# An eight-layer transformer block on one core: a deformable-attention loop's broadcasts, edge turns and warm-up matmuls reordered, and a product's last piece given to GpSimd

## The reference, cut to what matters

```python
x = x + _L0_xattn_ref(...)
...
x = x + _L2_xattn_ref(ctx_1024, ctx_1024, _layernorm(x, axis=-1), mask, Wk, bk, Wv, bv, Wq, bq, Woff, boff, Wo, bo)
...
x = x + _L3_ffn_ref(_layernorm(x, axis=-1), w_gate, w_up, w_down)
```

## Time and profile before

| | us |
|---|---|
| median of 3 runs | 460.71 (460.51 to 461.78) |
| the profiled execution, its own time | 460.47 |
| its span in the trace | 458.4 |
| PE busy | 396.8 |
| DVE busy | 360.2 |
| ACT busy | 253.6 |
| POOL busy | 111.7 |

### The profile page before, as it was taken

The page is one execution under the profiler, slowest core; times in us unless marked ns, Lnnn a source line. Parts: engine busy times, 40 slices in busy tenths (PEclk is TensorE's granted clock), DMA queues, the critical chain, the costliest instruction groups (busy, mean ns, idle before and its releaser), DMA issues.

```text
span 458.4 us, 8682 instructions
## 1 busy us (share of the span) xinstructions
PE 396.8 (87%) x3411; PEld 260.9 (57%) x3411; DVE 360.2 (79%) x807; ACT 253.6 (55%) x443; POOL 111.7 (24%) x92
## 2 busy tenths in 40 slices
PE   8988989999999988877787888899999999868156
PEld 5555556566666667643454555476656866643045
DVE  5799646548544487989699888998899799987985
ACT  4785753323223335377688785776667433444952
POOL 3200000006990001005993543131211023100200
PEclk9999999999999999999899999999999999989759
DMA  7990000000000000027000003000000000000001
GB/s 232 358 322 6 1 1 1 1 0 1 0 0 1 1 1 4 0 62 307 1 2 0 3 1 70 0 2 1 1 0 1 3 1 1 3 0 0 1 1 46
DMA packets 11084, 16.51 MB, mean 36 GB/s; under 512 B 5274, under 2 KB 9764, under 8 KB 10148
## 3 DMA queue, kind: packets, MB, share of 16 engines
q1 hardware_dynamic: 10756, 15.17, 9.5%
q10 hardware_dynamic: 288, 0.79, 0.5%
HBM read 15.43 MB, written 0.52 MB: 35 GB/s over the span
## 4 chain that ended last, share of the span: by engine, by line
PE 47%; DVE 34%; ACT 10%; issue 7%; DMA 1%; POOL 0%; ACTq 0%; DVEq 0%
PE ps L852 7%; PE ps L857 7%; PE ps L891 7%; PE ps L2156 5%; DVE arena L1937 3%; PE ps L2146 2%; PE ps L1786 2%; DVE stats L252 2%; DVE arena L2405 1%; DVE arena L2402 1%; DVE arena L610 1%; DVE arena L613 1%; PE ps L242 1%; DMA ctx_fm<-in_ctx_fm 1%; DVE arena L2433 1%
## 5 line engine op out<-in xcount | busy, mean ns | idle before, releaser
L970 DVE SCALAR_TENSOR_TENSOR arena<-ps,cols,arena 128x512 f32<-128x512 f32 x40 | 29.7, 750 | 42.3 <-PE ps L857 38.0
L866 ACT ACTIVATE arena<-ps,cols 128x512 f32<-128x512 f32 x40 | 27.4, 687 | 63.9 <-PE ps L852 63.8
L242 PE MATMUL ps<-const 128*128 128x256 f32 x158 | 42.2, 414 | 7.4 <-ACT arena L2746 4.4
L891 PEld LDWEIGHTS ps<-weights,arena 128*128 128x128 f32 x320 | 38.6, 192 | 8.1 <-issue 8.0
L1937 DVE TENSOR_SCALAR arena<-ps 128x512 f32<-128x512 f32 x56 | 36.4, 683 | 7.1 <-PE ps L1772 3.8
L242 PEld LDWEIGHTS ps<-const 128*128 128x128 f32 x158 | 30.8, 205 | 16.1 <-ACT arena L2746 4.7
L891 PE MATMUL ps<-weights,arena 128*128 128x128 f32 x320 | 39.2, 276 | 0.2 <-DVE x_tm L959 0.2
L857 PE MATMUL ps<-h_fm,weights 128*128 128x512 f32 x80 | 37.7, 593 | 0.7 <-DVE arena L970 0.7
L852 PE MATMUL ps<-h_fm,weights 128*128 128x512 f32 x80 | 37.7, 594 | 0.6 <-ACT h_fm L373 0.6
L2146 PE MATMUL ps<-h_fm,weights 128*128 128x512 f32 x64 | 30.3, 606 | 2.7 <-ACT arena L2530 1.8
L1772 PE MATMUL ps<-l2buf,picks_b 128*128 128x256 bf16 x160 | 25.6, 277 | 5.8 <-DVE arena L1937 4.8
(11 more groups left out here) (408 smaller groups left out, 884.4 us busy)
## 6 DMA issues: line engine op xcount, KB each, us to landing
weights<-in_moe_w SPq DMA_DIRECT2D x2, 2048.0 KB, 10.1
weights<-in_moe_w SPq DMA_DIRECT2D x3, 1280.0 KB
l2buf<-in_picks SPq DMA_DIRECT2D x1, 1664.0 KB, 7.6
rows<-in_rows SPq DMA_DIRECT2D x1, 1024.0 KB, 13.7
x_tm<-in_x SPq DMA_DIRECT2D x2, 256.0 KB, 5.0
ctx_fm<-in_ctx_fm ACTq DMA_DIRECT2D x1, 512.0 KB, 5.7
ctx_tm<-in_ctx SPq DMA_DIRECT2D x1, 512.0 KB, 14.5
mats<-in_mats SPq DMA_DIRECT2D x1, 512.0 KB, 14.8
```

The costliest lines, as they stand in the source:

```text
L242: PE.matmul(ps[:, bank, 0:256], ident, const[:, 0:256], start=True, stop=True)
L866: AC.activation(silu[:, k, :], ps[:, k, :], ACT.Silu, bias=bias_col(0, e, k)).then_inc(silu_ok, 1)
L891: ins = PE.matmul(ps[:, 4 + u % 2, P * t:P * t + P], glu[:, u % 2, k, P * t:P * t + P], w3[:, e, k, :], start=(k == 0), stop=(k == 1))
L970: V.scalar_tensor_tensor(out=glu[:, u % 2, k, :], in0=ps[:, 2 + k, :], scalar=bias_col(1, e, k), in1=silu[:, k, :], op0=ALU.add, op1=ALU.m ...
```

## The change

1. First attention: `stay_busy(pe, 2, 6)` is issued at t = 0 and at t = 1.
2. PE in the deformable loop: `sample(0)` comes after all five broadcasts of step 0. In step 1 the order is broadcast 5, one call of `stay_busy`, `move(2)`, broadcasts 6 to 9. The edge's turn comes after the step's broadcasts, just ahead of its `sample`.
3. ACT in the loop: `keep_positions(2)` comes ahead of the ramp of step 1; `keep_edge` comes after the ramps and `keep_values`.
4. DVE in the loop: the split of the third group of positions comes after hat 2 of step 0, ahead of hat 3.
5. Last product: ACT rounds in four pieces (512, 512, 1024, 1024 columns), and also subtracts the magic for the last 512 columns; POOL multiplies these 512 columns; DVE multiplies the other 2560 in four pieces and takes four maxima in all (the first two pieces in one). `gt_ok` reaches 6 after the third of four pieces, and the 8 calls of `stay_busy` start there.

```diff
-                    if t == 0:
+                    if t in (0, 1):
                         stay_busy(pe, 2, 6)
...
                     if w in MOVE_STEPS[3:]:
                         move(pe, MOVE_STEPS.index(w))
-                    if w in EDGE_STEPS:
-                        turn_edge(pe, EDGE_STEPS.index(w))
                     if w % 2 == 0 and chunks(w):
                         pe.wait_ge(ix_ok, w // 2 + 2)
                     for c in chunks(w)[:3]:
                         broadcast(w // 2 + 1, c)
-                    if w == 0:
-                        sample(0)
-                    if w == 1:
-                        move(pe, 2)
+                        if w == 1 and c == chunks(w)[0]:
+                            stay_busy(pe, 1, 6)
+                            move(pe, 2)
                     if w >= 2:
                         turn(w - 2)
                     for c in chunks(w)[3:]:
                         broadcast(w // 2 + 1, c)
+                    if w in EDGE_STEPS:
+                        turn_edge(pe, EDGE_STEPS.index(w))
+                    if w == 0:
+                        sample(0)
                     if 0 < w < NW:
                         sample(w)
...
-                    if w in EDGE_STEPS:
-                        keep_edge(act, EDGE_STEPS.index(w))
                     if 1 <= w <= NW:
                         to_sbuf(w - 1)
                     mine = [c for c in chunks(w) if is_act(c)]
+                    if w == 1:
+                        keep_positions(act, 2)
                     for c in mine:
                         ramp(w // 2 + 1, c)
                     if w >= 2:
                         keep_values(w - 2)
                     if w == 0:
                         spread_q(0)
-                    if w == 1:
-                        keep_positions(act, 2)
+                    if w in EDGE_STEPS:
+                        keep_edge(act, EDGE_STEPS.index(w))
...
                     for c in chunks(w)[2:4]:
                         hat(w // 2 + 1, c)
+                        if w == 0 and c == 2:
+                            dve.wait_ge(third_raw, 1)
+                            split_positions(V, dve_link, 1, slice(0, 4), third_ok)
...
-                    if w == 0:
-                        dve.wait_ge(third_raw, 1)
-                        split_positions(V, dve_link, 1, slice(0, 4), third_ok)
...
+            GS_PIECES, TAIL = ((0, 512), (512, 512), (1024, 1024), (2048, 1024)), 2560
+            TAIL_ROUNDED = NCH + len(GS_PIECES) + 1
...
-                for c in range(NCH):
-                    AC.activation(chunk(gate, c), chunk(gate, c), ACT.Identity, bias=magic, scale=inv[:, GS:GS + 1])\
-                        .then_inc(gt_ok, 1)
+                for start, n in GS_PIECES:
+                    v = gate[:, start:start + n]
+                    AC.activation(v, v, ACT.Identity, bias=magic, scale=inv[:, GS:GS + 1]).then_inc(gt_ok, 1)
+                act.wait_ge(gt_ok, NCH + len(GS_PIECES))
+                AC.activation(gate[:, TAIL:I3 * 8], gate[:, TAIL:I3 * 8], ACT.Identity, bias=minus_magic).then_inc(gt_ok, 1)
...
-                for c in range(NCH):
-                    dve.wait_ge(gt_ok, NCH + c + 1)
-                    dve_link(V.scalar_tensor_tensor(out=chunk(up, c), in0=chunk(gate, c), scalar=-MAGIC, in1=chunk(up, c),
-                                                    op0=ALU.add, op1=ALU.mult))
-                    ins = V.tensor_reduce(cm[:, c:c + 1], chunk(up, c), AX.X, ALU.max, apply_absolute_value=True)
+                dve.wait_ge(gt_ok, NCH)
+                for k, (start, n) in enumerate(GS_PIECES):
+                    n = min(n, TAIL - start)
+                    v, w = up[:, start:start + n], gate[:, start:start + n]
+                    dve.wait_ge(gt_ok, NCH + k + 1)
+                    ins = V.scalar_tensor_tensor(out=v, in0=w, scalar=-MAGIC, in1=v, op0=ALU.add, op1=ALU.mult)
+                    if k >= 1:
+                        dve_link(ins)
+                        ins = V.tensor_reduce(cm[:, k:k + 1], up[:, (0, start)[k > 1]:start + n], AX.X, ALU.max,
+                                              apply_absolute_value=True)
+                dve.wait_ge(gate1_ok, 2)
+                ins = V.tensor_reduce(cm[:, len(GS_PIECES):len(GS_PIECES) + 1], up[:, TAIL:I3 * 8], AX.X, ALU.max,
+                                      apply_absolute_value=True)
...
+                pool.wait_ge(gt_ok, TAIL_ROUNDED)
+                G.tensor_tensor(up[:, TAIL:I3 * 8], up[:, TAIL:I3 * 8], gate[:, TAIL:I3 * 8], ALU.mult).then_inc(gate1_ok, 1)
```

More of the change, by code:

```diff
@@ L2824, in _ @@
                 set_unit(dve, OUT, V.tensor_tensor(unit[:, OUT:OUT + 1], scl[:, GS:GS + 1], scl[:, UP:UP + 1], ALU.mult))
-                for c in range(NCH):
-                    dve.wait_ge(gt_ok, NCH + c + 1)
-                    dve_link(V.scalar_tensor_tensor(out=chunk(up, c), in0=chunk(gate, c), scalar=-MAGIC, in1=chunk(up, c),
-                                                    op0=ALU.add, op1=ALU.mult))
-                    ins = V.tensor_reduce(cm[:, c:c + 1], chunk(up, c), AX.X, ALU.max, apply_absolute_value=True)
+                dve.wait_ge(gt_ok, NCH)
[11 more added lines that the diff above has]
+                                      apply_absolute_value=True)
                 dve_link(ins)
-                V.tensor_reduce(amax, cm[:, 0:NCH], AX.X, ALU.max).then_inc(col_ok, 1)
+                V.tensor_reduce(amax, cm[:, 1:len(GS_PIECES) + 1], AX.X, ALU.max).then_inc(col_ok, 1)
                 all_max(dve, OUT)
@@ L2837, in _ @@
                 v = tokens(up, 128, 256)
-                dve.wait_ge(gt_ok, 2 * NCH + 1)
+                dve.wait_ge(gt_ok, TAIL_ROUNDED + 1)
                 V.tensor_scalar(v, v, -MAGIC, None, ALU.add).then_inc(o_ok, 1)
@@ L2841, in _ @@
                 V.tensor_scalar(last, last, -MAGIC, None, ALU.add).then_inc(o_ok, 1)
-                dve.wait_ge(gt_ok, 2 * NCH + 2)
+                dve.wait_ge(gt_ok, TAIL_ROUNDED + 2)
                 v = tokens(up, 512, 512)
```

## The result

The changed kernel took 458.64 us (median of 18 executions, 456.88 to 461.39). The kernel before, run as often beside it, took 461.99 (459.64 to 466.95), 1.3 more than the three runs that the prediction had. The ratio, which leaves a few disturbed executions out, is 0.9944, 95% interval 0.9924 to 0.9964: 0.56% or 2.6 us faster (the two medians with all executions in them are 3.35 apart). The whole interval lies beyond 0.3%. The forecast was 457.7, range 456.6 to 459.4. The median lies 0.9 above the forecast and inside the range; but on the level of before that the larger sample shows, the ratio gives 461.99 x 0.9944 = 459.4, which is on the range's upper edge. The profiled execution took 457.18, against 460.47: 3.3 us less.

A forecast was written before the change was run, and what follows sets the result against it. No engine alone was taken to bound the kernel: PE held 47% of the chain, DVE 34%. From 460.47, 1.8 us for the loop and 0.95 for the last product came off, giving 457.7 us, range 456.6 to 459.4.

The forecast's parts named there:

- DVE's first hat of step 2 at 225.7: Deformable loop: hat 0 of step 2 starts at 225.7 instead of 227.94, 2.25 us earlier.
- The head's calls: First attention: two more `stay_busy` calls cost PE 1.13 us, covered by an idle 1.26; taken as 0, at most 1.1.
- The loop's term: Deformable loop: net gain 1.8 us, from 2.4 less 0.6, bounds 0.3 and 2.6.
- 2.4 + 0.3: Loop: DVE's lead of 2.4 us at step 3, and the best bound, -0.3, for steps 8 and 12 together.
- I take 0.6: Loop, step 4: the edge now stands between the last broadcast and `sample(4)` and costs 0.6 us, bounds 0 and 0.67.
- I take 0 there and in step 12: Loop, steps 8 and 12: moving the edge gains and loses equally, net 0, bounds -0.3 and +0.6 together.
- The last product's term: Last product: gain 0.95 us, from start 0.5, DVE's sum 0.2 and earlier `stay_busy` calls 0.25; bounds 0 and 1.35.
- so 0.25 of the 0.35 is got back: Last product: `stay_busy` calls run 440.6 to near 446.3, so the last maximum's matmul is held up 0.25 us less.
- a fall in step 1: Rival, loop: the clock falls again in step 1, costing 1.65 us, 1.5 on the chain; total 459.2; chance 0.2.
- the starting value, 460.47: Whole kernel: the profiled execution's own time, from which the gains of 1.8 and 0.95 us were subtracted.
- I leave it out: Whole kernel: the 0.24 us by which the median of the runs lay above the profiled execution was not added.
- The prediction's 1.6: Last product: POOL's 512 columns take 1.6 us at least, up to 3.20, from 3.20 for 1024; 1.6 taken.

The follow-up runs named there:

- fill_more: The changed kernel with more `stay_busy` calls: two in the first mixture of experts, two and one in the queries ahead of the loop; median 457.50 us, ratio 0.9905 to before.

## Why the prediction was right and wrong

**Right: direction, mechanism, most of the steps.** The prediction had DVE's first hat of step 2 at 225.7. It came at 225.95, which is 225.73 on the time scale of before (less the 0.22 by which the first hat was late). `sample(1)` took 1.28 and started 0.15 later than forecast on that scale, at 223.97. The granted clock stayed 1.00 from 220 to 230. The head's calls cost nothing: the first expert starts at 52.06 with them and at 52.08 without. POOL was not waited for in the last product: its 512 columns took 1.27, beside a maximum of DVE's.

**The loop's term was too small: 1.8 forecast, 2.63 measured** (the stated bound was 2.6; the forecast's own terms, 2.4 + 0.3, allow 2.7). DVE's lead on the time scale of before, step by step: it was 2.5 at its first instruction on the keys (L1308), where 2.4 had been forecast, and 2.1 behind it. The two others on the keys, in step 3, brought it to 2.7. The lines before, then changed:

```profile
230.98 0.69 DVE L1308 TENSOR_SCALAR wn<-k_fm 128x1024 int32<-128x1024 f32 x1
...
234.90 1.02 DVE L1312 TENSOR_SCALAR h_fm<-k_fm 128x1024 f32<-128x1024 f32 x1
235.84 1.21 DVE L1313 TENSOR_SCALAR q_fm<-k_fm 128x1024 f32<-128x1024 f32 x1
```

```profile
228.71 1.07 DVE L1308 TENSOR_SCALAR wn<-k_fm 128x1024 int32<-128x1024 f32 x1
...
233.01 0.74 DVE L1312 TENSOR_SCALAR h_fm<-k_fm 128x1024 f32<-128x1024 f32 x1
233.67 0.88 DVE L1313 TENSOR_SCALAR q_fm<-k_fm 128x1024 f32<-128x1024 f32 x1
```

The prediction let DVE's instructions keep their durations. The same three took 2.92 before and 2.69 now, beside other instructions of POOL; no experiment shows that POOL is the reason. Two steps of the prediction failed besides. First, "I take 0.6" for step 4's edge: `sample(4)` came 2.1 earlier (2.3 without the late start), against the lead of 2.7 behind the keys; so it cost 0.4, and putting it back gave only 0.2. Secondly, "I take 0 there and in step 12": the lead grew from 2.3 to 2.45 in step 8 and to 2.6 in step 12. ACT's ramp no longer stands behind the edge's copy there, which fits, but these two steps were not tried alone.

**The last product's term was too large: 0.95 forecast, 0.54 measured.** The column came 0.79 earlier against a forecast of 0.7, with the start at 0.4 for 0.5 and DVE's sum at 0.4 for 0.2. What failed is "so 0.25 of the 0.35 is got back". Its own row gives less: 440.6 and the 5.90 of the earlier trace rows are 446.5, not 446.3. The calls start 3.2 earlier in the trace and end only 2.9 earlier, for they took 6.20, with the granted clock at 0.50 until 442 and 0.62 from there to 444. The maximum waited 1.34 us behind its column instead of 1.09: 0.25 lost, not gained. With 6 calls the wait is 0.74, and the term would have been 1.1.

**The clock was the right rival at the wrong place.** I gave 0.2 to a fall in step 1 and worked out 1.65 for it, 1.5 of it on the chain; it never came, and in the kernel before it costs 1.1 over the loop. What moved the executions instead are falls that the trace of before did not have, at 26, 92 and 212, which cost 2.2 to 2.5, 3.3 and 1.5 us. The step that failed is the starting value, 460.47, and with it "I leave it out", where the median of three runs stood 0.24 above the profiled execution: that took one execution for the level of all. Eighteen have their median at 461.99, 1.5 above it, and go up to 466.95. The changed kernel's fastest executions need 457.1 (seven of the eighteen lie between 456.9 and 457.4), its median is 0.9 above the forecast of 457.7. That the median falls inside the range is in part luck: the starting value was 1.5 too low, while the loop's term was 0.8 too small and the product's 0.4 too large.

By the Trainium skill (TensorE: Matmul & The Clock Gate, section A second HAM failure mode: psum-queue depth-cycling) the clock would fall and rise where banks are cycled with short idle spells. The traces agree for one stretch of the old order (four of four fall once, between 224 and 234). They disagree for the rest of its loop and for the new order, which cycle the same three banks at the same pace: from 234 to the join the granted clock stayed 1.00 in all four, and the new order never fell in thirteen traces.

**Left open.** Whether the call of `stay_busy` in step 1 and those in the head do anything. The loop of the kernel before without a fall is known from one trace that had two calls more, so how the loop's gain divides into clock and order is measured once. Whether the calls added in `fill_more` keep the clock is likely and not shown. And it is open why one DVE instruction on the keys (L1312) took 0.68 us in one trace and 1.19 in another.

## What to carry to other kernels

Cut the span at marks that both kernels have, and compare the pieces: the loop's piece repeated within 0.1 us, while whole executions scattered by 4 to 8. Compare only traces whose clock fell at the same places, the ones ahead of the piece too, for a fall there moved the loop's piece by 0.7 and the last product's by 0.5. Before a small change is priced, look at how a kernel's own executions scatter, and ask at which other places the clock can fall. Matmuls that are issued ahead of a matmul on the critical path only to keep PE busy need an end as well as a beginning: count them so that they are through, even with the clock at 1.2 GHz, when the critical matmul's input arrives.

## What the runs showed of the hardware that was not expected

- TensorE's clock fell while PE was mostly busy. Ahead of the fall at 92 PE was busy 3.28 of 4 us and idle 0.72 in one piece; the last work before it was transposes and matmuls that use 10 of the 128 columns or rows (`128*10` and `10*128` in the records of L912 and L917). Which of these matters is open, for in other traces the same work, with the same idle 0.72, kept 1.00. With two calls, 1.03 us, put into the idle time no trace of three fell there.
- The same program on the same chip took 456.9 to 461.5 us, and the traces differ by where the clock fell; the kernel before took 458.4 to 467.0 on the chips used, and 473 in two executions.
- POOL multiplied two tensors of 128x512 in 1.27 us beside DVE's maximum, and 128x1024 in 3.20, of which 1 us beside DVE's multiply of two tensors. The prediction's 1.6 had been called the least. But the trace of before had the same instruction on 128x1024 at 2.28 too, twice (L2312, at 384.30 and 389.80, beside DVE instructions that read at most one tensor in SBUF), and half of that is 1.14.
